# Graph layer on one core: message path on PSUM bank pairs instead of single banks

## What is computed

```
e        = relu(raw @ W_e1.T + b_e1) @ W_e2.T + b_e2
gated    = e * (clip(edge_attr[:, 0:1], 0, 1) + 0.01)
edge_emb = gated @ W_le.T + b_le
msg      = relu(h[src] + edge_emb)              # h = relu(layernorm(x))
aggr     = segment_sum(msg, dst)
out      = x + relu(layernorm((h + aggr) @ W_g1.T + b_g1) * ln_g + ln_b) @ W_g2.T + b_g2
```

## Time and profile before

| | us |
|---|---|
| median of 3 runs | 2256.02 (2248.27 to 2256.33) |
| profiled execution, its own time | 2254.22 |
| its span | 2252.5 |
| edge path, first to last gather issued | 72.0 to 2125.4 |
| busy PE, DVE, ACT, POOL | 2153.8, 2124.3, 2043.2, 1668.0 |

### The profile page before, as it was taken

One profiled execution on the slowest core, in us unless ns is written; L12 is line 12 of the kernel. 1 busy time (PEld: TensorE's weight loads), 2 busy tenths in 40 slices (PEclk: granted clock), 3 DMA queues, 4 the chain that ended last, 5 costly groups with the idle time before them and its releaser, 6 DMA issues. The chain is left out here.

```text
span 2252.5 us, 45214 instructions
## 1 busy us (share of the span) xinstructions
PE 2153.8 (96%) x14264; PEld 1950.4 (87%) x14264; DVE 2124.3 (94%) x4129; ACT 2043.2 (91%) x4668; POOL 1668.0 (74%) x1671
## 2 busy tenths in 40 slices
PE   3899999999999999999999999999999999999888
PEld 3788889898888989888898888989898888988787
DVE  8899999999999999999999999999999999999888
ACT  6799999999999999999999999999999999999754
POOL 7677777777777777777777777777777777777572
PEclk7899999999999999999999999999999999999989
DMA  9565656565656666666656566656565656666342
GB/s 302 134 159 152 160 150 160 150 160 151 158 152 161 156 157 158 154 157 152 157 154 157 152 154 156 160 152 160 152 158 151 161 154 157 155 157 155 94 132 96
DMA packets 138613, 349.55 MB, mean 155 GB/s; under 512 B 34113, under 2 KB 60674, under 8 KB 138370
## 3 DMA queue, kind: packets, MB, share of 16 engines
q0 software_dynamic: 77376, 211.39, 35.1%
q1 hardware_dynamic: 60994, 135.21, 23.8%
HBM read 333.64 MB, written 12.82 MB: 154 GB/s over the span
## 5 line engine op out<-in xcount | busy, mean ns | idle before, releaser
L540 POOL DMA_INDIRECT hx<-gather_table,sidx x1612 | 1563.3, 970 | 498.7 <-issue 491.0
L708 PE MATMUL bank<-wcr,hl 128*128 128x256 f32 x3224 | 906.1, 281 | 0.0
L706 PE MATMUL bank<-wcr,hh 128*128 128x256 f32 x3224 | 905.7, 281 | 0.0
L704 PE MATMUL bank<-wcr,hh 128*128 128x256 f32 x3224 | 904.1, 280 | 0.0
L625 DVE SCALAR_TENSOR_TENSOR bank<-bank,gt,hx 128x256 f32<-128x256 f32 x1612 | 676.6, 482 | 69.0 <-DMA hx<-gather_table,sidx 67.3
L704 PEld LDWEIGHTS bank<-wcr,hh 128*128 128x128 f32 x3224 | 608.6, 189 | 18.4
L706 PEld LDWEIGHTS bank<-wcr,hh 128*128 128x128 f32 x3224 | 607.4, 188 | 19.5
L708 PEld LDWEIGHTS bank<-wcr,hl 128*128 128x128 f32 x3224 | 607.1, 188 | 0.0
L562 ACT ACTIVATE mhl<-bank 128x512 fp32r<-128x512 f32 x806 | 483.8, 600 | 112.9 <-DVE bank L625 95.8
L635 DVE SCALAR_TENSOR_TENSOR mhl<-bank,mhl 128x512 fp32r<-128x512 f32 x806 | 519.4, 686 | 12.9 <-ACT mhl L562 0.3
L571 ACT ACTIVATE away<-iota,slot 128x128 f32<-128x128 f32 x1612 | 520.4, 409 | 0.0
(11 more groups left out here) (113 smaller groups left out, 1261.5 us busy)
## 6 DMA issues: line engine op xcount, KB each, us to landing
raw<-in_attrT SPq DMA_DIRECT2D x402, 256.0 KB
hx<-gather_table,sidx POOLq DMA_INDIRECT x1612, 2.8
x_sba<-in_x SPq DMA_DIRECT2D x12, 512.0 KB, 9.5
gather_table<-x_sba SPq DMA_DIRECT2D x12, 512.0 KB, 7.0
u_x<-in_x SPq DMA_DIRECT2D x12, 512.0 KB, 8.9
out<-u_x SPq DMA_DIRECT2D x12, 512.0 KB
dst_i<-in_dst_m SPq DMA_DIRECT2D x1, 805.5 KB
sidx<-in_src_m SPq DMA_DIRECT2D x1, 805.5 KB
```

Of the source, the lines that this page charges most:

```text
L540: eng.indirect_dma_start(out=hx[:, u % NX, j, :], out_offset=None, in_=tables, in_offset=bass.IndirectOffsetOnAxis(ap=sidx[:, t:t + 1], ax ...
L704: eng.matmul(o, hh[:, u % 2, k, e0:e0 + P], wcr[:, 0, k, :], start=False, stop=False, skip_group_check=seeded)
L706: eng.matmul(o, hh[:, u % 2, k, e0:e0 + P], wcr[:, 1, k, :], start=False, stop=False, skip_group_check=seeded)
L708: last = eng.matmul(o, hl[:, u % 2, k, e0:e0 + P], wcr[:, 0, k, :], start=False, stop=(j == 1 and k == 1), skip_group_check=seeded)
```

## The change

PSUM is declared as four tensors of two banks (`pair`), and the eight banks are views of these. `LA` is pair 0, and `LB` are pairs 1 and 2, one for a unit. hidden_high, hidden_low, message_high and message_low become one operation of 128x1024 each instead of two of 128x512, and r_hh, r_hl, r_mh and r_ml rise once a unit. total still has four operations of 256 columns, but raises r_t only after the last. seed writes c2 into both banks of the unit, 128x1024, so that from unit 2 on the matmul of L699 is gone; second_layer waits for the seed before its first matmul. r_l1 rises once, after both halves of first_layer. r_l2 still rises after each bank. Several waits that another wait implies are dropped: on r_l1 in raw_high, on the load in raw_low, on r_l2 in hidden_high and hidden_low, on r_sg in onehot_end and message_low, on r_hh in second_layer.

```diff
@@ -53,7 +53,8 @@
         def sem(name, c=ctx):
             return c.enter_context(nc.semaphore(name))
 
-        bank = [ctx.enter_context(nc.psum_tensor(f"bank{i}", [P, 512], F32)) for i in range(8)]
+        pair = [ctx.enter_context(nc.psum_tensor(f"pair{i}", [P, 2, 512], F32)) for i in range(4)]
+        bank = [pair[i // 2][:, i % 2, :] for i in range(8)]
...
@@ -397,12 +398,9 @@
 
         def raw_high(eng, u):
             loaded(eng, u)
-            if u >= NM:
-                eng.wait_ge(r_l1, 2 * (u - NM) + 2)
             eng.copy(rhi[:, u % NM, :], part(u)).then_inc(r_rh, 1)
 
         def raw_low(eng, u):
-            loaded(eng, u)
             eng.wait_ge(r_rh, u + 1)
             eng.tensor_tensor(rlo[F:P, u % NM, :], part(u)[F:P], rhi[F:P, u % NM, :].bitcast(F32),
                               ALU.subtract).then_inc(r_rl, 1)
@@ -518,10 +516,13 @@
                 r_su = sem("r_su", c)
                 r_tr = sem("r_tr", c)
                 r_ad = sem("r_ad", c)
-                LA = [bank[0], bank[1]]
-                LB = [bank[2], bank[3], bank[4], bank[5]]
+                LA = pair[0]
+                LB = [pair[1], pair[2]]
                 SG = [bank[6], bank[7]]
                 block = c.enter_context(nc.Block())
+
+                def message(u):
+                    return LB[u % 2][:, :, :].rearrange("p a (j n) -> p (a j) n", j=2)
...
@@ -534,7 +535,7 @@
                     eng.wait_ge(s_oa, 16 * len(NODE_GROUPS))
                     for u in range(UNITS):
                         if u >= NX and u % NW == 0:
-                            eng.wait_ge(r_t, 2 * (u + NW - 1 - NX) + 2)
+                            eng.wait_ge(r_t, u + NW - NX)
...
@@ -544,24 +545,19 @@
                 @block.scalar
                 def _(eng):
                     def hidden_high(u):
-                        if u >= 2:
-                            eng.wait_ge(r_l2, 2 * (u - 2) + 2)
-                        for k in range(2):
-                            eng.wait_ge(r_l1, 2 * u + k + 1)
-                            eng.activation(hh[:, u % 2, k, :], LA[k][:, :], ACT.Relu).then_inc(r_hh, 1)
+                        eng.wait_ge(r_l1, u + 1)
+                        eng.activation(hh[:, u % 2, :, :], LA[:, :, :], ACT.Relu).then_inc(r_hh, 1)
 
                     def seed(u):
-                        eng.wait_ge(r_ml, 2 * (u - 2) + 2)
-                        eng.copy(LB[(2 * u + 1) % 4][:, :].rearrange("p (j n) -> p j n", j=2),
-                                 c2[:, :].rearrange("p (a n) -> p a n", a=1).broadcast_to([P, 2, D])).then_inc(r_sd, 1)
-
-                    def message_high(u, q):
+                        eng.wait_ge(r_ml, u - 1)
+                        eng.copy(message(u), c2[:, :].rearrange("p (a n) -> p a n", a=1).broadcast_to([P, 4, D])
+                                 ).then_inc(r_sd, 1)
+
+                    def message_high(u):
                         if u >= 2:
                             eng.wait_ge(r_sg, u - 1)
-                        eng.wait_ge(r_t, 2 * u + q + 1)
-                        eng.activation(mh[:, u % 2, 2 * q:2 * q + 2, :],
-                                       LB[(2 * u + q) % 4][:, :].rearrange("p (j n) -> p j n", j=2),
-                                       ACT.Relu).then_inc(r_mh, 1)
+                        eng.wait_ge(r_t, u + 1)
+                        eng.activation(mh[:, u % 2, :, :], message(u), ACT.Relu).then_inc(r_mh, 1)
...
@@ -573,8 +569,6 @@
 
                     def onehot_end(u):
                         eng.wait_ge(r_aw, u + 1)
-                        if u >= 3:
-                            eng.wait_ge(r_sg, u - 2)
                         eng.activation(oh[:, u % 3, :, :], away[:, u % 2, :, :], ACT.Relu, bias=1.0,
                                        scale=-1.0).then_inc(r_oh, 1)
@@ -598,8 +592,7 @@
                             onehot(u + 1)
                             if u >= 1:
                                 seed(u + 1)
-                        message_high(u, 0)
-                        message_high(u, 1)
+                        message_high(u)
...
@@ -607,36 +600,28 @@
                 @block.vector
                 def _(eng):
                     def hidden_low(u):
-                        if u >= 2:
-                            eng.wait_ge(r_l2, 2 * (u - 2) + 2)
-                        for k in range(2):
-                            eng.wait_ge(r_hh, 2 * u + k + 1)
-                            eng.scalar_tensor_tensor(out=hl[:, u % 2, k, :], in0=LA[k][:, :], scalar=0.0,
-                                                     in1=hh[:, u % 2, k, :].bitcast(F32),
-                                                     op0=ALU.max, op1=ALU.subtract).then_inc(r_hl, 1)
+                        eng.wait_ge(r_hh, u + 1)
+                        eng.scalar_tensor_tensor(out=hl[:, u % 2, :, :], in0=LA[:, :, :], scalar=0.0,
+                                                 in1=hh[:, u % 2, :, :].bitcast(F32),
+                                                 op0=ALU.max, op1=ALU.subtract).then_inc(r_hl, 1)
 
                     def total(u):
-                        for q in range(2):
-                            eng.wait_ge(r_l2, 2 * u + q + 1)
-                            for j in range(2):
-                                t = 4 * u + 2 * q + j
-                                eng.wait_ge(r_hx[t % (4 * NX)], 16 * (t // (4 * NX) + 1))
-                                b = LB[(2 * u + q) % 4][:, D * j:D * j + D]
-                                last = eng.scalar_tensor_tensor(out=b, in0=b, scalar=gt[:, t:t + 1],
-                                                                in1=hx[:, u % NX, 2 * q + j, :],
-                                                                op0=ALU.mult, op1=ALU.add)
-                            last.then_inc(r_t, 1)
+                        for j in range(4):
+                            t = 4 * u + j
+                            if j % 2 == 0:
+                                eng.wait_ge(r_l2, 2 * u + j // 2 + 1)
+                            eng.wait_ge(r_hx[t % (4 * NX)], 16 * (t // (4 * NX) + 1))
+                            b = LB[u % 2][:, j // 2, D * (j % 2):D * (j % 2) + D]
+                            last = eng.scalar_tensor_tensor(out=b, in0=b, scalar=gt[:, t:t + 1],
+                                                            in1=hx[:, u % NX, j, :],
+                                                            op0=ALU.mult, op1=ALU.add)
+                        last.then_inc(r_t, 1)
 
                     def message_low(u):
-                        if u >= 2:
-                            eng.wait_ge(r_sg, u - 1)
-                        for q in range(2):
-                            eng.wait_ge(r_mh, 2 * u + q + 1)
-                            eng.scalar_tensor_tensor(out=ml[:, u % 2, 2 * q:2 * q + 2, :],
-                                                     in0=LB[(2 * u + q) % 4][:, :].rearrange("p (j n) -> p j n", j=2),
-                                                     scalar=0.0,
-                                                     in1=mh[:, u % 2, 2 * q:2 * q + 2, :].bitcast(F32),
-                                                     op0=ALU.max, op1=ALU.subtract).then_inc(r_ml, 1)
+                        eng.wait_ge(r_mh, u + 1)
+                        eng.scalar_tensor_tensor(out=ml[:, u % 2, :, :], in0=message(u), scalar=0.0,
+                                                 in1=mh[:, u % 2, :, :].bitcast(F32),
+                                                 op0=ALU.max, op1=ALU.subtract).then_inc(r_ml, 1)
...
@@ -679,26 +664,24 @@
                         eng.wait_ge(r_rl, u + 1)
                         if u == 0:
                             eng.wait_ge(r_one, 3)
+                        if u >= 1:
+                            eng.wait_ge(r_hl, u)
                         for k in range(2):
-                            if u >= 1:
-                                eng.wait_ge(r_hl, 2 * (u - 1) + k + 1)
-                            eng.matmul(LA[k][:, :], w1r[:, 0, k * P:k * P + P], rhi[:, u % NM, :], start=True, stop=False)
-                            eng.matmul(LA[k][:, :], w1r[:, 1, k * P:k * P + P], rlo[:, u % NM, :],
-                                       start=False, stop=True).then_inc(r_l1, 1)
+                            eng.matmul(LA[:, k, :], w1r[:, 0, k * P:k * P + P], rhi[:, u % NM, :], start=True, stop=False)
+                            last = eng.matmul(LA[:, k, :], w1r[:, 1, k * P:k * P + P], rlo[:, u % NM, :],
+                                              start=False, stop=True)
+                        last.then_inc(r_l1, 1)
 
                     def second_layer(u):
-                        eng.wait_ge(r_hh, 2 * u + 2)
-                        eng.wait_ge(r_hl, 2 * u + 2)
+                        seeded = u >= 2
+                        eng.wait_ge(r_hl, u + 1)
+                        if seeded:
+                            eng.wait_ge(r_sd, u - 1)
```

(13 more changed lines are left out.)

## The result

| | before | changed |
|---|---|---|
| median, us (4 runs each) | 2254.32 | 2298.48 |
| lowest to highest | 2248.27 to 2256.33 | 2293.75 to 2301.75 |
| span of the profiled execution | 2252.5 | 2300.0 |

The ratio is 1.0188 (1.0162 to 1.0213). The forecast was 2286.5, 30.5 more than the 2256.0 that was then known of the kernel before. The measured difference of the medians is 44.2.

What follows compares the result with a forecast made beforehand. The gathers on POOL were taken as the pace, 5.10 us a unit. A 5.08 loop through VectorE and ScalarE, 5.17 with windows, gave +29.5, the tail +1.0: 2256.0 + 30.5 = 2286.5 us, range 2253 to 2316.

Steps and rivals of the forecast that it cites:

- Its loop: total, message_high, message_low, hidden_low, next total stand in a row: 5.08 us a unit, 5.17 with windows; chance 0.72.
- The slopes: Wide operations priced from 512 to 1024 columns: 0.54 us more on VectorE, 0.42 on ScalarE; wide Relu 1.02.
- The hand-over of 0.03: VectorE's message_low starts 0.03 us after the end of ScalarE's Relu, message_high.
- the dropped waits: Waits on r_l1, r_l2, r_sg and the load, satisfied whenever a neighbouring wait is: bounds 0 to 0.03, taken as 0.
- its 0.09 from total to message_high: ScalarE's wide Relu starts 0.09 us after the end of VectorE's total; a term of the 5.08 loop.
- Unit 0: Start of the edge path: the first unit's total ends at 81.11 us, which nothing in the change alters.
- window_out: ScalarE's operation once in 7 units: takes up hidden_high's margin before hidden_low (1.95 against 2.20 us) and no more.
- The tail: After the last total, wide message_high and message_low take 2.4 us instead of 1.4: +1.0.
- Second seed and second_layer's wait: ScalarE's copy grows by 0.42 us, its loop 4.97 under 5.08; second_layer has over a us to spare: no cost.
- What would show it: Profile signs: VectorE idle 0.4 to 0.5 us a unit before message_low, some 180 in all; TensorE busy clearly less.
- POOL's waits for total: Sign: POOL waits for VectorE's total once in three units; forecast wrong if POOL still shows only "issue".
- faster, the gathers lose their long ones: Rival on POOL: raw_low no longer meets gather starts, -37 us with the tail, 2219; chance 0.04.

Runs made afterwards that it cites:

- a1: Kernel before with only message_high and message_low made wide and r_t raised once a unit; seed and hidden stay in halves: 2351.48 us, ratio 1.0398.
- a2: Changed kernel with message_high and message_low in halves again, r_t twice a unit; wide hidden and both seeds stay: 2253.20 us, ratio 0.9957.
- a3: Changed kernel with the seed of the second bank only, the first bank by the matmul as before: 2294.51 us, ratio 1.0147.
- a4: Kernel before with only the seven implied waits dropped: 2270.63 us, ratio 1.0053.
- w1: Changed kernel with message_low's implied wait on r_sg given back, on a slow chip: 3315.95 us against 3385.95 for the kernel before, ratio 0.9780.

## Why the prediction was right, and where its size was off

- *Its loop.* It held, mechanism and size. total, message_high, message_low, hidden_low: 5.08 forecast, 5.08 to 5.09 measured, and a1 and a2 show by adding and taking away the wide messages alone that this is the cause. The slopes held: the wide Relu took 1.027 us on average (1.02 forecast), wide message_low 1.225 (1.22).
- *The hand-over of 0.03.* It was read from a hidden_low that waited for one semaphore, and applied to message_low, which in the change too waits for one only. With the wait of before kept it would have been 0.11. The prediction put the dropped waits at 0; that was right for this sum only because the 0.03 was already that of a single wait. This was luck, for nothing in the prediction priced a second wait. In the same way its 0.09 from total to message_high was read from a message_high with two waits, and the change has two there as well. The step is not neutral: dropping message_low's second wait keeps about 32 us off the change (402 x 0.08, not measured as a time of its own).
- *Unit 0.* "Nothing changes" its total's end was wrong: +2.4. With an empty pipe, wide hidden operations come later than the first half of a pair, and second_layer waits for all of it; that is argued and not tested by itself. Without wide hidden operations, in a1, it was +1.1.
- *window_out.* The prediction said that it takes up ScalarE's margin and no more. hidden_high came 0.25 later, hidden_low started 1.19 after message_low instead of 1.14, and units with window_sum take 5.47 to 5.48, 0.39 more than clean ones where 0.32 was taken: 57 x 0.07 = 4 us. The last 2 us inside the loop are 402 x 0.005.

```profile
1028.10 1.22 DVE L622 SCALAR_TENSOR_TENSOR mhl<-pair,mhl 128x1024 fp32r<-128x1024 f32 x1 [0.43 <-ACT mhl L560]
1029.29 1.23 DVE L604 SCALAR_TENSOR_TENSOR hl<-pair,hh 128x1024 fp32r<-128x1024 f32 x1
1030.44 0.41 DVE L628 TENSOR_TENSOR agw<-agw,pair 128x256 f32<-128x256 f32 x1
```

- *The tail.* +1.0 forecast and measured. So up to the last message_low the forecast's 30.5 became 39.6; the remainder of the 44.2 lies in the stretch behind, which differs between executions as said above.
- *Second seed and second_layer's wait.* Covered, as forecast, by a3. TensorE waits for the seed 276 times, 71.7 us, and nobody waits for TensorE.
- *What would show it.* The hole before message_low (0.4 to 0.5, some 180 us) came out as 0.43 and 174.0. TensorE was to be "clearly less" busy and was so by 24.0 of 2153.8 us. POOL's waits for total did not come, and the prediction had named just that as a sign of being wrong. What failed is the sign and not the loop: it took for granted that a queue that is faster than VectorE must in the end wait for a buffer, though the rows of a held gather stood in the same prediction. The rival "faster, the gathers lose their long ones" was based on a true row, but the change made four times as many long gathers, not fewer.
- *That the gathers pace the kernel before* rests on VectorE's 84 waits for landings (67.3 us) and on POOL's row; no run on an ordinary chip has tested it, and a row of gathers without a hole has turned out to prove little by itself.

## What to carry to other kernels

Merging two half-size operations saves a fixed cost on each engine, here 0.11 us a unit on VectorE, but where one half's successor on another engine ran under the second half, the merge lays that successor open: sum the loop through both engines before merging, and merge only where the two engines don't alternate (wide messages alone cost 4.0% here, about 1.4% of it by the double wait, and the change without them was 0.4% faster than before). Drop waits that another implies on the instruction that takes over from another engine in the critical loop; elsewhere it gained nothing here (a4 was 0.5% slower). A queue that never waits is not thereby the pace: compare its free step with its actual one, and see who holds it. And before a run on another chip is compared, look at its granted clock: eight runs here tell little of the time at 2255 us.

## What was not expected of the hardware

- A VectorE instruction with two waits started 0.11 us after the release by ScalarE, one with a single wait 0.03 (a1 and w1 against the change and a3), though the second semaphore was long there. On ScalarE, released by VectorE, it was 0.09 against 0.035.
- A gather issued by POOL while VectorE ran a 64x512 operation on two SBUF tensors ended 0.81 to 0.84 us after that operation, instead of 0.95 after its own start, in each of the 2332 cases that all the traces hold; with that operation at 16 columns it happened once. A gather that started up to 0.04 us after the operation wasn't held, and the operation was longer instead, 0.72 to 0.77 against 0.69. Two engines without a common semaphore went in step through it.
- The same program took 2254 and 2260 us on ordinary chips and 3289 and 3386 us on two others. In the traces from those two, TensorE stood still again and again with nothing to wait for, and its granted clock then fell to half, for 1017 to 1178 us of the edge path with all gathers.
